# A sandwich of Nystrom attention and a routed expert layer: bias products moved into the expert loop, products of zeros added at three places

## The reference

```python
# attention: batch 0 alone gives the Nystrom output that is added to every batch
xg = nystrom_attention(dense, qkv_w, out_w, out_b, conv_w)   # 8 heads, 32 landmarks, 6 inverse iterations
enc = xg[0] + dense
q, k = enc @ wq, enc @ wk
data = (q @ k.T)[0] / sqrt(32)
A_raw = segment_sum(adj_vals * data[adj_rows, adj_cols], adj_rows)   # 16384 edges
alpha = softmax(A_raw)
value = dense @ wv_w + wv_b
xl = alpha[:, None] * value
sw = sigmoid(-xl) ** 2
xo = xl * 2 * sw + 2 * enc * (1 - sw)
# experts: 16 experts, the best 4 of each token
logits = -dist2(x, keys) + x @ rw.T + rb
topv, topi = top_k(logits, 4); w = softmax(topv)
hidden = gelu(x @ w1[e].T + b1[e])
out = sum over the 4 chosen e of  w[e] * (hidden @ w2[e].T + b2[e])
```

## Time and profile before

| | |
|---|---|
| runs of the kernel before | 589.01, 590.24, 591.65 us |
| profiled execution, its own time | 585.99 us |
| its span, first to last instruction | 584.3 us |
| PE busy | 501.3 us (86%) |
| DVE, ACT, POOL busy | 354.3, 353.1, 282.4 us |
| mean granted TensorE clock | 0.929 |

### The profile page before, as it was taken

The page is one execution under the profiler, slowest core; times in us unless marked ns, Lnnn a source line. Parts: engine busy times, 40 slices in busy tenths (PEclk is TensorE's granted clock), DMA queues, the critical chain, the costliest instruction groups (busy, mean ns, idle before and its releaser), DMA issues.

```text
span 584.3 us, 18669 instructions
## 1 busy us (share of the span) xinstructions
PE 501.3 (86%) x6226; PEld 464.5 (80%) x6226; DVE 354.3 (61%) x1302; ACT 353.1 (60%) x1067; POOL 282.4 (48%) x309
## 2 busy tenths in 40 slices
PE   3989978999826056999989999999999999999963
PEld 3975868999814043999989999999998999999722
DVE  6563666999889963667587787122235664442136
ACT  5723316777574643665686998666766666666404
POOL 5000010000005615776777777777777777777700
PEclk9999996999966557999999999999999999999978
DMA  8974000000070023675667776776698977687382
GB/s 242 255 228 191 3 3 3 0 0 0 1 288 1 1 90 107 189 204 167 176 182 188 196 264 177 206 215 182 178 269 268 288 227 199 201 234 225 101 289 74
DMA packets 55738, 92.19 MB, mean 158 GB/s; under 512 B 10352, under 2 KB 26096, under 8 KB 55152
## 3 DMA queue, kind: packets, MB, share of 16 engines
q1 hardware_dynamic: 45424, 72.35, 40.9%
q0 software_dynamic: 10240, 18.89, 11.4%
HBM read 78.07 MB, written 17.37 MB: 163 GB/s over the span
## 4 chain that ended last, share of the span: by engine, by line
PE 65%; DVE 15%; issue 6%; ACT 6%; DMA 4%; POOL 3%; DVEq 1%; POOLq 0%; SPq 0%; ACTq 0%
PE bank L2177 23%; PE bank L2184 21%; DVE shared L1212 3%; PE bank L2169 2%; DVE shared L1204 2%; PE bank L1771 2%; PE bank L2106 2%; DMA shared<-yd 2%; DMA yd<-value_early 2%; POOL yd L610 2%; PE bank L1876 2%; PE bank L1808 1%; PE bank L1798 1%; PE bank L2039 1%; PE bank L2122 1%
## 5 line engine op out<-in xcount | busy, mean ns | idle before, releaser
L908 ACT ACTIVATE value_early<-bank,shared 128x128 f32<-128x128 f32 x632 | 180.7, 369 | 96.8 <-PE bank L2177 95.4
L2177 PE MATMUL bank<-value_early,shared 128*128 x1264 | 170.2, 278 | 4.2 <-ACT value_early L916 3.6
L2184 PE MATMUL bank<-shared,value_early 128*128 x1264 | 167.4, 275 | 2.2 <-ACT value_early L908 2.2
L2177 PEld LDWEIGHTS bank<-value_early,shared 128*128 128x128 f32 x1264 | 154.9, 193 | 7.4 <-issue 7.3
L2184 PEld LDWEIGHTS bank<-shared,value_early 128*128 128x128 f32 x1264 | 154.0, 192 | 2.6 <-issue 2.6
L602 POOL DMA_INDIRECT shared<-xd,value_early x128 | 125.5, 980 | 56.1 <-issue 31.7
L610 POOL DMA_INDIRECT yd<-value_early x128 | 126.8, 991 | 40.6 <-issue 28.7
L1695 DVE SCALAR_TENSOR_TENSOR value_early<-bank,value_early 128x128 f32 x158 | 54.8, 347 | 88.5 <-PE bank L2184 76.1
L572 POOL TENSOR_TENSOR shared<-shared,xn 128x512 f32<-128x512 f32 x4 | 5.1, 1267 | 96.3 <-DVE xn L1288 89.9
L2039 PE MATMUL bank<-ksp,shared 128*128 128x32 bf16 x1536 | 41.1, 178 | 0.0
L2039 PEld LDWEIGHTS bank<-ksp,shared 128*128 128x128 bf16 x1536 | 40.3, 97 | 0.1
(11 more groups left out here) (341 smaller groups left out, 699.7 us busy)
## 6 DMA issues: line engine op xcount, KB each, us to landing
shared<-w1b SPq DMA_DIRECT2D x158, 258.0 KB
w1b<-in_w_t SPq DMA_DIRECT2D x1, 4096.0 KB
shared<-col_dram SPq DMA_DIRECT2D x1, 4096.0 KB
shared<-in_w_t SPq DMA_DIRECT2D x1, 4096.0 KB
att<-yd SPq DMA_DIRECT2D x8, 512.0 KB, 5.7
shared<-yd SPq DMA_DIRECT2D x4, 1024.0 KB, 9.1
xd<-xnT SPq DMA_DIRECT2D x2, 1280.0 KB, 5.1
shared<-xd,value_early POOLq DMA_INDIRECT x128, 3.7
```

Of the source, the lines that this page charges most:

```text
L908: ins = act.activation(hT[:, i % 2, tok(c)], bank[2 + i % 2][:, tok(c)], ACT.Gelu, bias=w1_now[:, i % WR, F + c:F + c + 1])
L2177: ins = mm(bank[2 + i % 2][:, tok(c)], w1_now[:, i % WR, tok(c)], x_now, start=True, stop=True)
L2184: ins = mm(bank[6 + i % 2][:, 0:D], hT[:, i % 2, tok(c)], w2_sb[:, bass.ds(e, 1), c, :] .rearrange("p a d -> p (a d)"), start=(c == 0), st ...
```

## The change

Five edits:

- The zeros that `idle` multiplies are written by DVE as its first instruction, not by POOL among the constants, and have a semaphore of their own. DVE's small identities follow the statistics of batch 0.
- PE multiplies zeros 18 times ahead of its first wait for the constants, three times after each of batches 0 and 1, and once after each of batches 2 and 3.
- ACT loads the table of the square root before it waits for the first statistics.
- PE multiplies zeros 24 times between `prefix(0)` and `table(0)`.
- `gates_T(0)`, the four `bias_rows` of the first half and ACT's five copies leave the list: PE's stand behind steps 3, 5, 7, 9 and 11 of the loop, ACT's behind steps 4, 6, 8, 10 and 12. The four products now share bank 5, so each waits for the copy of the one ahead. PE's wait for the gates' copy ahead of the loop is gone.

```diff
--- before.py
+++ after.py
@@ -292,6 +292,7 @@
             "r_ps", "r1_ready", "r3_ready", "s3_ps", "s3_max", "p3_ready", "p3T_ps", "p3T_ready", "a3v_ps", "a3v_ready")]
         xnT_odd, p1_ready, p1T_ps, p1T_ready = [sem(s) for s in ("xnT_odd", "p1_ready", "p1T_ps", "p1T_ready")]
         xT_ready = sem("xT_ready")
+        zeros_ready = sem("zeros_ready")
         band_ps, band_ready = sem("band_ps"), sem("band_ready")
         xT_ps, max_ready, max_ps, ohr_act = [sem(s) for s in ("xT_ps", "max_ready", "max_ps", "ohr_act")]
         pz_ps, t_ready, pzT_ready, tz_ps, zn_ps, z_ready, zT_ready = [sem(s) for s in (
@@ -361,7 +362,7 @@
             return bank[b % 2] if b < BH else bank[5]
 
         def bias_bank(q):
-            return bank[2 + 4 * (q % 2)] if q < 4 else bank[4]
+            return bank[5] if q < 4 else bank[4]
 
         def of_steps(eng, row, i, most):
             at = i // NI * P + i % NI
@@ -522,7 +523,6 @@
             pool.memset(eps_c[:, 0:1], EPS)
             pool.memset(eps_c[:, 1:2], EPS / 4)
             pool.memset(zero_r[:, :], 0.0)
-            pool.memset(zeros[:, :], 0.0)
             pool.iota(iota_e[:, :], pattern=[[1, E]], base=0, channel_multiplier=0,
                       allow_small_or_imprecise_dtypes=True)
             step(pool.memset(blk_l[:, :], 1.0))
@@ -681,6 +681,7 @@
                 act.wait_ge(xnT_ps, b + 1)
                 act.activation(xnT[:, b * N:(b + 1) * N], bank[b % 2][:, :], ACT.Copy).then_inc(xnT_ready, 1)
 
+            table(1, ACT.Sqrt)
             deviation(0)
             for b in range(B):
                 if b + 1 < B:
@@ -878,14 +879,14 @@
             target_parts()
             for t in range(TS):
                 numbered(t)
-                if t == TS // 2 - 1:
+            table(2, ACT.Gelu)
+
+            def prepare(i):
+                if i == 4:
                     gT_copy(0)
-            for q in range(BH):
-                bias_copy(q)
-            table(2, ACT.Gelu)
-
-            def prepare(i):
-                if i in (15, 17, 19, 21):
+                elif i in (6, 8, 10, 12):
+                    bias_copy((i - 6) // 2)
+                elif i in (15, 17, 19, 21):
                     x2T_copy(BH + (i - 15) // 2)
                 if i == 30:
                     gate_exp(1)
@@ -984,13 +985,16 @@
                                 in1=wvb_row[:, :].unsqueeze(1).broadcast_to([P, NT, D]), op=ALU.add)\
                  .then_inc(val_ready, 1)
 
-            dve.wait_ge(const_ready, 1)
-            step(v.tensor_reduce(out=ident_c[:, :], in_=ident[:, :].rearrange("p (h j) -> p j h", j=L), axis=AX.X,
-                                 op=ALU.add))
-            for n, c in enumerate((7.0, 15.0)):
-                ins = v.tensor_scalar(identw[:, n, :, :], ident_c[:, :].unsqueeze(1).broadcast_to([P, G2, L]), c, None,
-                                      ALU.mult)
-            ins.then_inc(xT_ready, 1)
+            v.memset(zeros[:, :], 0.0).then_inc(zeros_ready, 1)
+
+            def identities():
+                dve.wait_ge(const_ready, 1)
+                step(v.tensor_reduce(out=ident_c[:, :], in_=ident[:, :].rearrange("p (h j) -> p j h", j=L), axis=AX.X,
+                                     op=ALU.add))
+                for n, c in enumerate((7.0, 15.0)):
+                    ins = v.tensor_scalar(identw[:, n, :, :], ident_c[:, :].unsqueeze(1).broadcast_to([P, G2, L]), c, None,
+                                          ALU.mult)
+                ins.then_inc(xT_ready, 1)
 
             def stats_of(b):
                 dve.wait_ge(x_in[loaded(b)], 16)
@@ -1001,6 +1005,7 @@
                 v.tensor_copy(xnT[:, b * N:(b + 1) * N], bank[1][:, :]).then_inc(xnT_odd, 1)
 
             stats_of(0)
+            identities()
             for b in range(1, 6):
                 stats_of(b)
                 batch_norm(b - 1)
@@ -1776,6 +1781,8 @@
                 for _ in range(n):
                     mm(bank[at][:, :], zeros[:, 0:P], zeros[:, :], start=True, stop=True)
 
+            pe.wait_ge(zeros_ready, 1)
+            idle(18, 2)
             pe.wait_ge(const_ready, 1)
 
             def band_product(c):
@@ -1810,6 +1817,8 @@
                     ins.then_inc(xl_ps, 1)
                 if b >= 2:
                     value_product(b - 2)
+                if b < NT:
+                    idle(3 if b < 2 else 1, 4)
 
             def v_product(t):
                 if t < 2:
@@ -2118,7 +2127,7 @@
                     .then_inc(gT_ps, 1)
 
             def bias_rows(q):
-                pe.wait_ge(gT_ready, max(q, 1) if q < 4 else q + 2)
+                pe.wait_ge(gT_ready, q + 1 if q < 4 else q + 2)
                 mm(bias_bank(q)[:, :], gT[:, q % 4 // 2, :], b2_bd[:, (q % 2) * 512:(q % 2 + 1) * 512],
                    start=True, stop=True).then_inc(gT_ps, 1)
 
@@ -2131,18 +2140,17 @@
             router(BH - 1)
             pe.wait_ge(const_ready, 3)
             prefix(0)
+            idle(24, 7)
             for t in range(TS):
                 table(t)
-                if t == TS // 2 - 1:
+            step_experts(0)
+
+            def prepare(i):
+                if i == 3:
                     gates_T(0)
-                elif t in (TS - 5, TS - 3):
-                    bias_rows((t - TS + 5) // 2)
-            step_experts(0)
-            for q in range(2, BH):
-                bias_rows(q)
-
-            def prepare(i):
-                if i in (14, 16, 18, 20):
+                elif i in (5, 7, 9, 11):
+                    bias_rows((i - 5) // 2)
+                elif i in (14, 16, 18, 20):
                     b = BH + (i - 14) // 2
                     x2_T(b)
                     if b > BH:
@@ -2189,7 +2197,6 @@
             pe.wait_ge(w_in, 48)
             for n in range(brought(0)):
                 rows_T(n)
-            pe.wait_ge(gT_ready, 5)
             e_now, at_now = [], slots(pe, 0)
             for i in range(IALL):
                 up(i, at_now.pop(0))
```

More of the change, by code:

```diff
@@ L880, in _ @@
                 numbered(t)
-                if t == TS // 2 - 1:
-                    gT_copy(0)
-            for q in range(BH):
-                bias_copy(q)
             table(2, ACT.Gelu)
             def prepare(i):
-                if i in (15, 17, 19, 21):
+                if i == 4:
+                    gT_copy(0)
+                elif i in (6, 8, 10, 12):
+                    bias_copy((i - 6) // 2)
+                elif i in (15, 17, 19, 21):
                     x2T_copy(BH + (i - 15) // 2)
```

## The result

| | before | changed |
|---|---|---|
| first comparison, median (range, runs) | 589.83 us (589.01 to 591.65, 4) | 583.15 us (582.67 to 583.88, 4) |
| its ratio, with 95% interval | | 0.9884 [0.9857, 0.9911] |
| repeated later, median (range, runs) | 587.29 us (583.32 to 591.15, 23) | 583.33 us (581.90 to 586.05, 12) |
| its ratio, with 95% interval | | 0.9947 [0.9915, 0.9980] |
| profiled execution, its span | 585.99, 584.3 us | 583.56, 581.7 us |

A ratio here is estimated from the single runs, so it is not the quotient of the two medians and can differ from it by up to 0.0024. By how much the kernel is faster depends on the runs of before: over the 87 of the three later series it ranges from 582.56 to 592.71 us (medians 587.18, 587.29 and 586.66), and the four of the first comparison all lay in its upper part.

The account below looks back on a forecast made before the run. PE was taken to bound most of the start, the list's end and the loop to step 18, POOL behind it. -3.9 - 5.2 + 3.7 + 1.0 = -4.4: 581.6 us profiled, 585.8 us median; range 581.5 to 590.5.

Parts of the forecast that it names:

- Table: End of the list: without gates and bias products the table ends at 217.5, near the slow-clock end, against 222.73; -5.2 us.
- The rival in which the zeros overrun the table: Ahead of the table: the 24 zeros all run slow, so it starts at 211.4; 588.0 us in all, chance 0.13.
- Loop: Loop before step 18: two transposes and four bias products of 0.86 us stand in PE's chain; +3.7 us.
- The rival by which they cost nothing: Loop: the bias products are free because POOL is nearly full; 582.1 us in all, chance 0.13.
- Clock at the loop's start: First blocks behind the gathers: nothing fills PE, so one more block runs slow; +1.0 us, between 0 and +2.8.
- Start: Up to the queries' products: early table load gains 0.5 us, zeros hold the fast clock; 27.1 instead of 30.98, -3.9 us.
- The carry to a median of 590.24: Whole kernel: the median's 4.25 us above the profiled execution's 585.99 us is added to the forecast.
- The clock falls again before batch 0: Start: the clock drops in the gap behind the zeros, start gives about 0; 589.7 us in all, chance 0.17.
- The zeros make it slower: Start: clock falls, zeros between batches cost PE time, up to two more batches slow; +4.5, 594.7 us, chance 0.07.

Follow-up runs that it names:

- experiment 2: Changed kernel without any products of zeros; moved gates and bias products, early square-root table and DVE's memset stay: 585.01 us, ratio 0.9962 to the kernel before.
- experiment 3: Changed kernel without the 24 products of zeros ahead of the table: 586.48 us, ratio 0.9976 to the kernel before.
- experiment 1: Kernel before with only the start part of the change (list and loop as before, no 24 zeros): 585.84 us, ratio 1.0001.
- experiment 4: Changed kernel without the 26 zeros of the start, the 24 kept; timed twice: 586.74 us, ratio 1.0007, and 584.80 us, ratio 0.9963, to the kernel before.
- experiment 5: The changed kernel itself, unaltered, timed again in 12 runs: 583.33 us, ratio 0.9947 to the kernel before.
- experiment 6: Changed kernel with the 4 MB copy of the first expert weights issued behind the broadcast of the columns: 584.82 us, ratio 0.9959 to the kernel before.
- experiment 7: Changed kernel with 14 products of zeros ahead of the batches instead of 18; one profiled execution, 586.72 us.
- experiment 8: Changed kernel with the gates' transposes and four pairs of bias products put between the table and the gathered rows; one profiled execution, 581.88 us.
- experiment 10: Changed kernel with gates and bias products between table and gathered rows, and the first expert weights' copy behind the broadcast: 579.19 us, ratio 0.9877 to the kernel before.
- late copy: Changed kernel's 4 MB copy of the first expert weights issued behind the broadcast of the columns; alone ratio 0.9959 to the kernel before.
- experiment 9: Changed kernel with gates' transposes and bias products between the table and the gathered rows, timed in 12 runs: 580.55 us, ratio 0.9920 to the kernel before.

## Why the prediction held, and where it did not

The time, 583.2, lies in the predicted range and 2.6 us below the forecast of 585.8, and faster was the likeliest verdict. Of the four terms two were right, one had the wrong sign, and one was right where it was measured and gone 25 us later.

*Table: -5.2 forecast, -5.06 measured, right.* The products of a group didn't wait for the clock, and ACT's numbering didn't hold them. The row list stands 8.16 us behind the table's first product (8.19 without zeros, experiment 2). The reason given for staying near the slow end, that the clock would be low, was only half true: it was high for the first two microseconds, and the products ran at the same pace. The rival in which the zeros overrun the table did not come about, since they ended 1.6 us early. Their lifting of the clock was worth nothing to the table, as experiment 3 shows.

*Loop: +3.7 forecast, right.* Four pairs of 0.86 us and two transposes of 0.22 are 3.66, and each stands in the chain at the step predicted. The rival by which they cost nothing is excluded: POOL waits for them.

*Clock at the loop's start: +1.0 forecast, -1.0 measured.* This term had the wrong sign. The row list to the fourth scatter took 2.66 us longer, not 3.66 + 1.0. I had argued that without the bias products as filling more blocks would be slow. The first block behind the fourth gather took 1.42 us, where it had taken 1.81, and the next was already at 0.89. The second `up` block behind the gather starts 12.52 us behind the row list and not 13.51, which is the 1.0 us; 0.27 of it is that the gather landed earlier, and the rest is the clock. Over other executions it is less: row list to fourth scatter is 53.03 us in experiment 1, with the old placement, and 55.87 to 56.26 in experiments 2 to 5, with the new one, so the term lies between -1.0 and -0.4. Stretches of 1 us at that place, in the trace of before:

```profile
232.00:233.00 1.00, 0.35 (x2) 0.32 (x2) 0.00 (x0) 0.85 (x4) 0.70 (x2) 0.53 0.32 84
...
235.00:236.00 1.00, 1.00 (x9) 1.00 (x9) 0.65 (x5) 1.00 (x5) 0.86 (x1) 0.76 0.41 116
```

and in the changed kernel's:

```profile
228.00:229.00 1.00, 1.00 (x6) 1.00 (x6) 0.68 (x2) 0.78 (x4) 0.95 (x1) 0.50 0.33 88
229.00:230.00 1.00, 1.00 (x11) 1.00 (x10) 0.53 (x4) 0.42 (x2) 0.70 (x1) 1.00 0.39 68
```

In before the clock had risen at about 221.8 us, behind the first two pairs of bias products, fallen at 225.2, risen at 228.7 while PE waited for the gather, and fallen again at 232.1, just ahead of the first block; it came back at 235.5. Experiment 1, with the old placement, does the same (down 231.4, up 234.8). In the changed kernel it rises once, at 229.0, and stays, and so in experiments 2, 4 and 5. PE was busy for only 3.4 of the 6.8 us of before's two high stretches; the rest fell into waits.

*Start: -3.9 forecast, -4.0 measured at the queries' products, +0.3 at the prefix.* This is the step that failed. Its working held: transposes at 9.14 against 9.3, fast from batch 0, and the queries' products at 26.82 against 27.1. What failed is the sentence left unsaid, that what PE gains at 27 us it keeps to the end. PE then stood from 34.25 us on for 3.30 us, waiting for no semaphore, and the clock fell, for 7 us. From the start of the cut products to the value products behind them it took 4.87 us (33.86 to 38.73), where before took 0.99 (37.94 to 38.93), and from there to the products of L1878 5.64, where it was 4.74. The two losses are 3.88 and 0.90 us, together 4.8: the gain of 4.0 and the 0.85 us by which the convolution comes later. Experiment 1 shows the loss by itself (ratio 1.0001, -4.0 us at 27 us and +0.6 at 52). Experiments 6 and 7 show where the break comes from: a packet of instructions that comes 2.3 us later when the copy of the weights fills the engines, and a break that moves with the instruction count.

That is only a part of the loss. In experiment 6 the break is 2.4 us shorter and the convolution 2.0 us earlier, but of the 4.4 us by which PE leads before at the sixteen products (33.56 against 37.94) it still keeps 1.1. What goes is the remaining 0.92 us and, for the most part, slow products: 2.05 us for two at L1795 where before (L1788) has 1.10, and 3.12 for four at L1878 where before (L1869) has 1.88. So most of what is left of the loss is the clock, and why it falls is not shown. In all nine traces with zeros at the start there is a break and the clock falls between 35.2 and 41.7 us; in the five without them neither happens, and once it has risen the clock stays up until 84 us. Experiments 8 and 4 bring PE to the queries at the same time (31.66 and 31.67), and the clock falls only in 8, which has the break. Against the break as the whole cause: the clock fell behind 0.92 us in experiment 6 and behind 0.85 in experiment 10, and it stayed up through the new break of 2.38 us at 59 us. And in all seven traces in which the zeros held it, it fell 30.7 us after it had risen, whatever the length of the break. It isn't a fixed time after the rise either, since in experiments 7 and 8 it was 20.5 us and without the zeros 58 us or more. No experiment has the zeros without a break.

Why the total came out lower than forecast all the same is a matter of sums. From the trace's own time the forecast was -4.4 and the traces gave -2.4, which is the start's 3.9 missing and the loop's 2.0 better. The carry to a median of 590.24 added 4.25 us, and later runs put before at 587, so two errors of some 2 us and 3 us went against each other. That the prediction's 585.8 was close is partly luck. As a ratio it said 0.9925, which is inside the interval of the repeat and outside that of the first comparison.

*The rivals.* "The clock falls again before batch 0" happens in experiment 8, and in 7 with its fourteen, but not in the seven other traces with eighteen. Eight executions can't give its share. "The zeros make it slower" has been seen in small: in these two the queries' products come at 31.66, 0.8 us later than in the profiled execution of before, and the convolution 2.2 and 3.9 us later. It has not been seen in a median. The convolution starts between 51.82 and 53.15 in five traces with the zeros and the early copy, at 53.75 and 55.45 in the two that lost the clock, and between 50.20 and 56.45 in the five without zeros. The means of the first five and of the last five are 52.4 and 52.2, and with the one that lost the clock the eighteen zeros have 52.6. The zeros may narrow the spread, and the mean doesn't move.

The late copy's new break (59 to 62 us), and whether a copy placed elsewhere would avoid both, was not tried.

## What to carry to other kernels

Time gained early counts only when its next consumer is followed too: carry each gain to the first mark behind which both traces run alike, and look there for what the earlier arrival will run into. Marks further on say less: from the convolution to the prefix no kernel but those with the late copy differs, and still the twelve other traces need between 146.4 and 148.6 us. Work that must be done on the bounding engine belongs where that engine waits for a transfer anyway: two pairs of bias products cost 3.6 us among the table's, and all four pairs with the gates' transposes 3.7 in the loop and at most 1.4 in the gap between. Before paying for products of zeros, compare the duration of the products behind them at both levels of the clock, since those of the table don't depend on it.

## What was not expected of the hardware

- PE can stand for 0.85 to 3.93 us with no semaphore and no engine to wait for. A packet of 0.02 MB on an instruction queue precedes its return by 2.3 to 2.9 us in each of the nine traces with the break. It competes with ordinary copies: with the engines full it came at 34.8 us, with them empty at 32.5. That the packet is PE's, and that PE stood because its instructions were late, is inferred from this and from the break's move in experiment 7; the profile doesn't name it.
- The table's products take 0.127 us each at a granted clock of 1.00 and of 0.50 alike. Their weight loads are read with a stride, those of the second half aren't, and the grouped view of the changed kernel shows the difference (us in all, mean ns of one, idle before):

```profile
L2115 PEld LDWEIGHTS bank<-value_early 128*128 128x128 f16 x64 | 7.9, 148 | 2.1 <-ACT value_early L843 2.1
L2115 PEld LDWEIGHTS bank<-xnT 128*128 128x128 f16 x64 | 3.9, 98 | 1.2 <-issue 1.0
```

- At this change of ACT's table its load is all that the timeline shows: the last numbering ends at 215.55 us, the load follows, and the next instruction comes 0.02 us behind it.

```profile
215.57 1.28 ACT L661 ACT_TABLE_LOAD   x1
216.87 0.20 ACT L661 ACTIVATE of_table<-eps_c 128x1 f32<-128x1 f32 x1
```

The Trainium skill ("ScalarE: Activation LUTs", section "What ACT_TABLE_LOAD costs") counts a drain of about the same length on top. Neither ahead of the load nor behind it does the trace show it here.

- Executions of the same instructions differ at the start by what the clock does: with the same 18 zeros the queries' products began at 26.82 us in experiment 9 and at 31.66 in experiment 8, which is the same kernel.
